# Softmax denominators in an attention and expert kernel: VectorE folds moved sums into GpSimd's partial sum, and TensorE's sum stands later

## The reference

```
x = x + attention(ctx, layernorm(x))       # causal mask: key index <= query index, softmax over keys
x = x + ffn(layernorm(x))                  # sigmoid encoder, 8 experts, top 2, sigmoid, decoder, layernorm
```

## Time and profile before

| | us |
|---|---|
| three runs, median (lowest to highest) | 2900.06 (2897.03 to 2902.71) |
| the profiled execution | 2903.43 |
| its span in the profile | 2901.8 |
| PE busy | 2803.8 (97%) |
| DVE busy | 1873.2 (65%) |
| POOL busy | 1570.4 (54%) |
| ACT busy | 1521.4 (52%) |

### The profile page before, as it was taken

One profiled execution on the slowest core, in us unless ns is written; L12 is line 12 of the kernel. 1 busy time (PEld: TensorE's weight loads), 2 busy tenths in 40 slices (PEclk: granted clock), 3 DMA queues, 4 the chain that ended last, 5 costly groups with the idle time before them and its releaser, 6 DMA issues. The chain is left out here.

```text
span 2901.8 us, 42115 instructions
## 1 busy us (share of the span) xinstructions
PE 2803.8 (97%) x15464; PEld 1655.4 (57%) x15464; DVE 1873.2 (65%) x3483; ACT 1521.4 (52%) x2904; POOL 1570.4 (54%) x717
## 2 busy tenths in 40 slices
PE   8989999999999999999999999999889999999996
PEld 7877555555555555555554555553576666655653
DVE  4367888886688876778876788860663544344544
ACT  3232456666566667566666566666334343444332
POOL 0000377888678888677888678888661210111110
PEclk9998899999999999999999999999999999999998
DMA  6568456668746778756778656677693110011000
GB/s 243 188 195 245 127 143 152 152 154 186 176 134 157 160 161 190 182 138 153 159 162 193 161 146 139 146 165 193 194 315 117 44 34 26 30 44 44 30 29 15
DMA packets 138708, 407.89 MB, mean 141 GB/s; under 512 B 11632, under 2 KB 28528, under 8 KB 111888
## 3 DMA queue, kind: packets, MB, share of 16 engines
q0 software_dynamic: 32272, 226.77, 33.2%
q1 hardware_dynamic: 101056, 169.07, 20.3%
q10 hardware_dynamic: 5184, 9.44, 1.0%
HBM read 114.33 MB, written 70.78 MB: 64 GB/s over the span
## 5 line engine op out<-in xcount | busy, mean ns | idle before, releaser
L1063 DVE TENSOR_REDUCE row_max<-m_bank 128x1 f32<-128x512 f32 (+4 forms) x2240 | 1254.1, 624 | 269.1 <-PE m_bank L1168 171.5
L1046 ACT ACTIVATE pT<-s_bank 128x512 f32<-128x512 f32 (+5 forms) x2176 | 1085.6, 578 | 621.6 <-PE s_bank L1213 444.6
L986 POOL TENSOR_TENSOR part_sum<-part_sum,pT 128x2048 f32<-128x2048 f32 (+1 forms) x252 | 1032.7, 4098 | 159.0 <-ACT pT L1046 150.8
L1213 PE MATMUL s_bank<-q_sb,k_sb 104*128 104x512 f32 (+3 forms) x2176 | 841.0, 411 | 12.6 <-ACT pT L1046 7.5
L1168 PE MATMUL m_bank<-k_sb,q_sb 96*128 96x512 f32 (+4 forms) x2240 | 843.9, 410 | 8.7 <-DVE den L1090 3.1
L1168 PEld LDWEIGHTS m_bank<-k_sb,q_sb 96*128 96x128 f32 x2240 | 432.3, 196 | 209.3 <-DVE row_max L1063 127.2
L1213 PEld LDWEIGHTS s_bank<-q_sb,k_sb 104*128 104x128 f32 x2176 | 411.5, 192 | 215.4 <-ACT pT L1046 124.4
L1230 PE MATMUL o_bank<-pT,v_sb 128*32 128x512 f32 (+5 forms) x4352 | 497.3, 574 | 0.0
L1639 POOL TENSOR_TENSOR f_var_eps<-f_mean_var,eps 128x4 f32<-128x4 f32 x8 | 1.6, 202 | 474.0 <-DVE f_mean_var L1858 474.0
L1230 PEld LDWEIGHTS o_bank<-pT,v_sb 128*32 128x32 f32 (+1 forms) x4352 | 113.3, 109 | 229.2 <-ACT pT L1046 112.2
L986 POOL TENSOR_TENSOR part_sum<-pT 128x2048 f32<-128x2048 f32 x28 | 127.8, 4565 | 134.9 <-ACT pT L1046 134.9
(11 more groups left out here) (198 smaller groups left out, 3378.4 us busy)
## 6 DMA issues: line engine op xcount, KB each, us to landing
moved_sum<-pT POOLq DMA_DIRECT2D x208, 1024.0 KB, 7.3
q_sb<-qT_hi SPq DMA_DIRECT2D x64, 256.0 KB, 5.1
k_sb<-kT_hi SPq DMA_DIRECT2D x48, 256.0 KB, 9.5
x_in<-in_x SPq DMA_DIRECT2D x8, 1024.0 KB, 6.1
qT_hi<-q_hi SPq DMA_DIRECT2D x8, 1024.0 KB, 4.2
qT_lo<-q_lo SPq DMA_DIRECT2D x8, 1024.0 KB, 6.5
q_sb<-qT_lo SPq DMA_DIRECT2D x32, 256.0 KB, 4.7
aT<-o_sb ACTq DMA_DIRECT2D x32, 256.0 KB, 5.3
```

What stands on the lines that cost most here:

```text
L986: pool.tensor_tensor(total, pT[:, slot(S - 1), :, q0:] if j and kt == 1 else total, pT[:, slot(S), :, q0:], ALU.add).then_inc(pool_added, 1)
L1046: act.activation(pT[0:rows, slot(S), h, q0:], s_bank[(HG * S + h) % S_RING][0:rows, q0:], ACT.Exp, scale=SCALE).then_inc(exp_done, 1)
L1063: dve.tensor_reduce(row_max[:, j % 2, r, h, c:c + 1], m_bank[p % M_BANKS][:, 0:n], AX_X, ALU.max).then_inc(unit_max, 1)
L1213: mm = pe.matmul(out[:, q0:], k_sb[0:R_END, h, at:at + P], q_sb[query_buffer(g, j)][0:R_END, h, q0:], start=True, stop=kt < 4 * j)
```

## The change

For blocks 1 to 6 VectorE adds chain 0 of `moved_sum` into `part_sum` (`fold`); in blocks 5 and 6 it adds both chains. That is 32 adds of 128x2048 elements, at 24 places. In VectorE's order a fold stands behind everything of step 1 of the next block, and it waits for all of GpSimd's adds of its block and for the chain's DMAs. TensorE leaves out the matmuls of the folded chains, and waits for the fold before it sums `part_sum`. Its sum stands behind step 4 of the next block and not behind step 2 (blocks 0 and 7 keep 2). A folded chain is started anew once it has been folded, not once the block's sum is done. `STORE` goes from 7 to 6, and the planner is given `T_FOLD` for a fold.

```diff
-DEN_AFTER, INVERT, SPREAD, NORMALISE, STORE = 2, 1, 2, 3, 7
-SUMS_BEHIND = {ST * g + FIRST_STEP[j + 1] + DEN_AFTER: (g, j) for g in range(NG) for j in range(QB) if (g, j) != (NG - 1, QB - 1)}
+DEN_AFTER, INVERT, SPREAD, NORMALISE, STORE = 4, 1, 2, 3, 6
+SUMS_BEHIND = {ST * g + FIRST_STEP[j + 1] + (DEN_AFTER if 0 < j < QB - 1 else 2): (g, j)
+               for g in range(NG) for j in range(QB) if (g, j) != (NG - 1, QB - 1)}
+FOLD_AFTER = 1
+def folded_chains(g, j):
+    if j in (0, QB - 1):
+        return ()
+    return range(CHAINS) if j >= 5 else range(1)
...
+FOLDS_AT = {ST * g + FIRST_STEP[j + 1] + FOLD_AFTER: (g, j) for g, j, _ in FOLDS}
...
+T_FOLD = 2.35
...
+        if h == HG - 1 and S in FOLDS_AT:
+            x = x._replace(dve=max(x.dve, end) + T_FOLD * len(folded_chains(*FOLDS_AT[S])))
...
-                        reach(pool, block_done, QB * g + (j if j > 1 else 0))
+                        if (*previous_chains(g, j), c) in FOLD_NUMBER:
+                            reach(pool, folded, FOLD_NUMBER[(*previous_chains(g, j), c)])
+                        else:
+                            reach(pool, block_done, QB * g + (j if j > 1 else 0))
...
+                def fold(g, j):
+                    reach(dve, pool_added, PO * g + PO_BEFORE[FIRST_STEP[j + 1]])
+                    for c in folded_chains(g, j):
+                        reach(dve, moved[c], 16 * (TR[c] * g + TR_BEFORE[c][FIRST_STEP[j + 1]]))
+                        reach(dve, folded, FOLD_NUMBER[g, j, c] - 1)
+                        dve.tensor_tensor(part_sum[:, j % 2], part_sum[:, j % 2], moved_sum[:, c], ALU.add).then_inc(folded, 1)
...
-                    for c in range(CHAINS) if j else ():
+                    chains = [c for c in range(CHAINS) if j and c not in folded_chains(g, j)]
+                    for c in chains:
...
+                    if folded_chains(g, j):
+                        reach(pe, folded, FOLD_NUMBER[g, j, folded_chains(g, j)[-1]])
                     for h in range(HG):
-                        mm = pe.matmul(out[h], ones[:, :], part_sum[:, j % 2, h], start=j == 0, stop=not direct)
+                        mm = pe.matmul(out[h], ones[:, :], part_sum[:, j % 2, h], start=not chains, stop=not direct)
```

More of the change, by code:

```diff
@@ L536, with previous_chains @@
 TR = [TR_BEFORE[c][ST] for c in range(CHAINS)]
-DEN_AFTER, INVERT, SPREAD, NORMALISE, STORE = 2, 1, 2, 3, 7
-SUMS_BEHIND = {ST * g + FIRST_STEP[j + 1] + DEN_AFTER: (g, j) for g in range(NG) for j in range(QB) if (g, j) != (NG - 1, QB - 1)}
+DEN_AFTER, INVERT, SPREAD, NORMALISE, STORE = 4, 1, 2, 3, 6
[6 more added lines that the diff above has]
+    return range(CHAINS) if j >= 5 else range(1)
+FOLDS = [(g, j, c) for g in range(NG) for j in range(QB) for c in folded_chains(g, j)]
+FOLD_NUMBER = {fold: n + 1 for n, fold in enumerate(FOLDS)}
+FOLDS_AT = {ST * g + FIRST_STEP[j + 1] + FOLD_AFTER: (g, j) for g, j, _ in FOLDS}
+def previous_chains(g, j):
+    return (g, j - 1) if j > 1 else (g - 1, QB - 1)
 def max_units(j):
@@ L670, in sums_time @@
             return 0
-        j = SUMS_BEHIND[2 * v][1]
+        g, j = SUMS_BEHIND[2 * v]
         own = sum(widths(j, kt) for kt in range(key_tiles(j)) if adder(j, kt) == "matmul")
-        return T_VALUES * (1 + (CHAINS if j else 0) + own) + T_TURN
+        return T_VALUES * (1 + (CHAINS - len(folded_chains(g, j)) if j else 0) + own) + T_TURN
     def slot_free(self, x, S):
@@ L862, in attend @@
         p_used = t.sem("p_used")
+        folded = t.sem("chains_folded")
         pool_added, moved = t.sem("pool_added"), [t.sem(f"moved_sum_added{c}") for c in range(CHAINS)]
@@ L1122, in _ @@
                         spread(*SUMS_AT[S - SPREAD])
+                    if S in FOLDS_AT:
+                        fold(*FOLDS_AT[S])
                     if vector_adds(g, j, kt):
@@ L1186, in denominators @@
                     out = [m_bank[p % M_BANKS][h * HD:(h + 1) * HD, :] for h in range(HG)]
-                    for c in range(CHAINS) if j else ():
+                    chains = [c for c in range(CHAINS) if j and c not in folded_chains(g, j)]
+                    for c in chains:
                         reach(pe, moved[c], 16 * (TR[c] * g + TR_BEFORE[c][FIRST_STEP[j + 1]]))
                         for h in range(HG):
-                            pe.matmul(out[h], ones[:, :], moved_sum[:, c, h], start=c == 0, stop=False)
+                            pe.matmul(out[h], ones[:, :], moved_sum[:, c, h], start=c == chains[0], stop=False)
                     direct = [kt for kt in range(key_tiles(j)) if adder(j, kt) == "matmul"]
                     reach(pe, pool_added, PO * g + PO_BEFORE[FIRST_STEP[j + 1]])
+                    if folded_chains(g, j):
+                        reach(pe, folded, FOLD_NUMBER[g, j, folded_chains(g, j)[-1]])
                     for h in range(HG):
-                        mm = pe.matmul(out[h], ones[:, :], part_sum[:, j % 2, h], start=j == 0, stop=not direct)
+                        mm = pe.matmul(out[h], ones[:, :], part_sum[:, j % 2, h], start=not chains, stop=not direct)
                     for kt in direct:
```

## The result

The changed kernel takes **2994.3 us** (median of 4 runs, 2991.7 to 3000.3) against 2901.4 before: a ratio of 1.032, 95% interval 1.030 to 1.033. The forecast was 2992. The parts behind that sum are less exact than the sum, as the experiments show.

The account below looks back on a forecast made before the run. TensorE, busy 97% of the span, was taken to bound the kernel. Removed sets, waits and lower clock gave 2903.4 - 27.5 + 82 + 38 = 2995.9 us for the profiled execution, 2992 as a median; range 2900 to 3020.

Parts of the forecast that it names:

- What bounds, and what is removed: In attention: TensorE bounds, busy 436 of 440 us; leaving out 32 chain sets of 0.86 us saves 27.5 us.
- What the fold meets: In step 1 of the next block: VectorE arrives 0.2 to 1.2 us late and must wait out GpSimd's add, at 23 places.
- the ties: Passages from block 6 to 7: VectorE and GpSimd arrive almost together; if VectorE wins, GpSimd's add goes between the two folds.
- the last passage of group 3: Group 3's last block change, with no units left: VectorE was claimed free in time, so this place was not counted.
- the 23: Places in attention where a fold was claimed to meet GpSimd's add: 16 with one fold, 7 with two.
- What waits for it: TensorE, behind the folds: waits of 3.6 us at 16 places and 3.4 at 7, together 82 us more.
- the example: Passage from block 3 to 4: fold ends at 457.90, TensorE's fifth unit comes at 454.8 and waits 3.7 us.
- The clock: Behind TensorE's waits in attention: a fall to 1.2 GHz loses 1.65 us at each of 23 places, 38 us more.
- The sum: Whole kernel: 2903.4 - 27.5 + 82 + 38 = 2995.9 us for the profiled execution, 2992 as a median.
- rival 3: At the folds in attention: TensorE's waits come but its clock stays up; 2954 us, chance 0.20.
- Rival 1: At the folds: no exclusion that matters, the fold runs beside or before GpSimd's add; 2873 us, faster, chance 0.17.

## Why the prediction was right

- **What bounds, and what is removed.** Right: 32 sets went. Measured in medians, the kernel without the folds' adds is 14 to 15 us faster than before, not 27.5. The step that failed is "The planner's new order outside these places is taken as equally good, to within 3 us": it cost 12 to 14, some 11 of them in lower clock.
- **What the fold meets.** Right in mechanism and size: the fold ended 6.72 us behind the add's start for 6.71 worked out, late by 0.57 for 0.6; the ties went as described. The prediction called VectorE free in time in the last passage of group 3; that was so for the first fold there (2.29 us) and not for the second (6.45), and no unit or sum of the 23 waited for it. With one input the whole effect is gone.
- **What waits for it.** Right in places (16 units, 7 sums), too high in size: 61 us for 82. The folds' ends were right, so it was TensorE's own way that was counted too short. At the example it came to the fifth unit 4.4 us behind the start of GpSimd's add, for 3.6 worked out with items 0.23 apart, and waited 3.0 us for 3.7. Seven other units waited 2.4 to 2.5. Five of the sums were reached 6.7 to 6.8 us behind that start, for 5.7; and two, from block 6 to 7, only at 8.3, since they stand behind all four scores of step 4 (in the example from block 5 to 6 they stand behind one), and waited only 1.1 to 1.2.
- **The clock.** Right, and too low: 45 to 50 us for 38. I had 1.65 at each place; there was nothing at four, and 3.4 at five. That the falls come behind waits of 2.5 us as well, no row of mine had shown: the one of 2.57 had none.
- **The sum.** The terms as measured are -27.5 + 14 + 61 + 45 = 92.5, for 92.9 in all. They are differences between runs that follow on each other, so that they add up proves nothing; the recorded waits and clocks (61.5 and 43 of 105.7) are what bears it out. Forecast was -27.5 + 82 + 38 = 92.5. Two terms too low (by 14 and 7) and one too high (by 21) cancelled: that the number came out to 2 us is luck, the direction and the mechanism are not. Without the clock term, which came from two rows of another stage, the forecast would have been rival 3's 2954, 40 us off.
- **Rival 1** named the point that decides: whether VectorE reaches the fold before GpSimd's add. One step earlier it does, and 107 us are gone.

## What to carry to other kernels

An operation that fits by its length and by both engines' shares can still cost many times its length if it meets a long instruction of an engine that excludes it; ask what the other engine runs at that moment, and move it into that engine's idle time (here one step, 107 us) before giving it more room. Price a wait of the matmul engine with what follows it: here 61 us of waits brought 45 us or more of lower clock. And a planner that moves other work to make room has a price of its own, here 12 to 14 us, that a run with the operation left out shows.

## What the runs showed of the hardware

An exclusion lasts through a GpSimd add of 4.57 us: 5.7 to 6.5 us for an add of VectorE that takes 2.29 alone, and in the other direction 6.68 for 4.57. Where the add of GpSimd came first, the end of VectorE's was set by it alone: 6.72 to 6.75 us behind its start, for 0.27 to 1.07 us of lateness. A reduction over the same 2048 elements with one SBUF input took 2.27 to 2.29 at the same places, and a transpose from SBUF to SBUF 0.70 inside such an add. Of 21 waits of TensorE of 2.4 to 3.4 us, 19 came with a fall to the lower clock, which lost 1.7 or 3.4 us of work; the longest wait did not. Eight units in a row at VectorE's pace, with one wait of 0.74 us, brought a fall that lost 5.1 us. Keeping TensorE at work through the 23 waits, on results that nobody reads, made the kernel 45 us faster.
